# Routing 4,096 tokens to eight experts: one-hot marks made eight picks at a time, router weights held stationary

## The reference, cut to what matters

```python
logits = jnp.einsum('btc,ce->bte', x, router_w) + router_b      # 8 experts, x layer-normalised
top_k_logits, expert_indices = jax.lax.top_k(logits, 2)
expert_probs = jax.nn.softmax(top_k_logits, axis=-1)
one_hot = jax.nn.one_hot(ei, E, dtype=jnp.int32)                # ei: first picks of all tokens, then second
pos = jnp.cumsum(one_hot, axis=0) * one_hot - 1                 # slot of a pick in its expert
expert_inputs = buf.at[ei.ravel(), pos.ravel()].add(xr)         # 1,228 slots for each expert
```

## Time and profile before

| | |
|---|---|
| median of three runs | 2324.01 us |
| the profiled execution, its own time | 2329.72 us |
| its span, first to last instruction | 2328.0 us |
| PE, PEld, DVE, ACT, POOL busy | 2073.9, 1804.6, 1274.3, 1189.6, 500.8 us |
| TensorE clock granted, mean over the span | 0.95 |

### The profile page before, as it was taken

One profiled execution on the slowest core, in us unless ns is written; L12 is line 12 of the kernel. 1 busy time (PEld: TensorE's weight loads), 2 busy tenths in 40 slices (PEclk: granted clock), 3 DMA queues, 4 the chain that ended last, 5 costly groups with the idle time before them and its releaser, 6 DMA issues.

```text
span 2328.0 us, 39168 instructions
## 1 busy us (share of the span) xinstructions
PE 2073.9 (89%) x14589; PEld 1804.6 (78%) x14592; DVE 1274.3 (55%) x2694; ACT 1189.6 (51%) x1926; POOL 500.8 (22%) x728
## 2 busy tenths in 40 slices
PE   5479999999996899999999999984799999999990
PEld 5258888888986678888888788872598899988890
DVE  4555555555555557575575764735445554555544
ACT  1145556655653656465565664611446655675530
POOL 5621111011102212022021100136211101111327
PEclk9999999999998899999999999965799999999995
DMA  5122321222122000000000000030222221222214
GB/s 159 44 77 84 99 79 65 75 86 93 48 89 63 26 8 20 5 15 15 6 19 8 13 1 1 2 126 3 77 58 72 90 72 47 87 95 86 73 59 145
DMA packets 84179, 133.18 MB, mean 57 GB/s; under 512 B 10200, under 2 KB 65824, under 8 KB 84064
## 3 DMA queue, kind: packets, MB, share of 16 engines
q1 hardware_dynamic: 69472, 94.67, 12.1%
q0 software_dynamic: 14592, 36.93, 5.7%
HBM read 98.84 MB, written 32.70 MB: 57 GB/s over the span
## 4 chain that ended last, share of the span: by engine, by line
PE 76%; PEld 7%; POOL 7%; DVE 3%; issue 3%; ACT 2%; DMA 1%; PEldq 1%; DVEq 0%; SPq 0%; POOLq 0%
PE bank L598 28%; PE bank L617 12%; PE bank L669 12%; PE bank L762 4%; PEld bank L617 4%; POOL route_space L450 4%; PEld bank L598 3%; PE bank L745 3%; PE bank L695 3%; PE bank L750 3%; PE bank L717 3%; PE bank L564 2%; POOL halves L466 2%; PE bank L730 2%; PE bank L704 1%
## 5 line engine op out<-in xcount | busy, mean ns | idle before, releaser
L598 PE MATMUL bank<-halves 128*128 128x512 f32 (+2 forms) x3744 | 774.4, 367 | 22.8 <-DVE halves L1186 22.8
L598 PEld LDWEIGHTS bank<-halves 128*128 128x128 f32 x3744 | 651.6, 191 | 129.8 <-issue 25.1
L617 PE MATMUL bank<-halves 128*128 128x256 f32 (+1 forms) x3288 | 403.1, 283 | 3.1 <-issue 3.1
L617 PEld LDWEIGHTS bank<-halves 128*128 128x128 f32 (+1 forms) x3288 | 397.3, 189 | 5.8 <-issue 4.9
L856 ACT ACTIVATE temp<-bank,bias_now 128x512 f32<-128x512 f32 (+1 forms) x312 | 200.2, 642 | 372.4 <-PE bank L598 372.1
L431 POOL DMA_INDIRECT wide<-normed,spare x160 | 164.6, 1029 | 901.0 <-PE bank L579 859.3
L1199 DVE SCALAR_TENSOR_TENSOR temp<-bank,bias_fc,temp 128x512 f32<-128x512 f32 (+1 forms) x312 | 216.1, 693 | 230.1 <-ACT temp L856 226.5
L669 PE MATMUL bank<-halves 128*128 128x512 f32 x1152 | 285.7, 399 | 3.3 <-DVE halves L1327 2.0
L1206 DVE TENSOR_TENSOR halves<-temp,halves 128x512 fp32r<-128x512 f32 (+1 forms) x312 | 198.0, 635 | 126.4 <-ACT halves L815 123.4
L815 ACT ACTIVATE halves<-bank 128x512 fp32r<-128x512 f32 (+1 forms) x176 | 90.1, 545 | 330.0 <-PE bank L579 215.4
L669 PEld LDWEIGHTS bank<-halves 128*128 128x128 f32 x1152 | 211.9, 189 | 51.3 <-DVE halves L1327 2.4
(11 more groups left out here) (174 smaller groups left out, 2338.0 us busy)
## 6 DMA issues: line engine op xcount, KB each, us to landing
expert_out<-rows SPq DMA_DIRECT2D x144, 128.0 KB, 1.7
wide<-in_L_ffn_w_c_fc SPq DMA_DIRECT2D x16, 1024.0 KB, 5.6
wide<-in_L_ffn_w_gate SPq DMA_DIRECT2D x16, 1024.0 KB, 7.6
wide<-in_L_ffn_w_c_proj SPq DMA_DIRECT2D x16, 1024.0 KB, 5.4
normed<-wide SPq DMA_DIRECT2D x8, 1024.0 KB, 4.4
x<-in_L_attn_x SPq DMA_DIRECT2D x4, 1024.0 KB, 9.5
out_x<-x SPq DMA_DIRECT2D x32, 128.0 KB, 2.4
wide<-normed,spare POOLq DMA_INDIRECT x160, 2.8
```

Source lines behind the costliest of these rows:

```text
L598: m = pe.matmul(bank[at + b][:, 0:w], a[:, kc, j * P:(j + 1) * P], v[:, kc, 0:w], start=(i == 0), stop=(i == len(ps) - 1))
L617: mm = pe.matmul(bank[4 + t % 2][0:m, 0:C], a[:, j, o:o + m], v[:, j, :], start=(k == 0), stop=(k == len(ps) - 1))
```

## The change

It does three things.

- **Normalising** is all VectorE's, batch by batch, as soon as a batch's reciprocal is there; `by_pool` and `wait_normed` go. `set_constants` (three memsets) moves ahead of the batches. ScalarE takes the third batch's root one supertile earlier.
- **Logits**: the router's weights are the stationary operand (128x8, two halves of the channels) and the turned tokens move, 512 columns at a time, into an [8, 512] result. ScalarE copies that to `logits_by_expert`, and TensorE turns it back tile by tile to the old place. The turn of supertile s-1 is issued behind the logits of s.
- **Marks**: `row16` and `list16` are the row and the list in bfloat16. Eight picks at a time, VectorE compares lists (`here`, 8x80) and rows (`by_row`, 8x128) and multiplies `here` with the tile's number; ScalarE multiplies `here` with the row's own number. TensorE waits once for eight picks.

The diff, cut to its core:

```diff
-                    for s in (2 * q, 2 * q + 1):
-                        wait_normed(sp, r, s)
+                    sp.wait_ge(xn_made, r * TILES + (q + 1) * QT)
...
-                    for i in range(first, first + tiles):
-                        if by_pool(r, i // SUPER):
-                            nc.gpsimd.tensor_scalar(xn[:, i, :], x[:, i, :], stats[:, i, 1:2], rstd[:, i:i + 1],
-                                                    ALU.subtract, ALU.mult).then_inc(xn_made_pool, 1)
...
-                for j in range(PICKS):
-                    nc.gpsimd.tensor_scalar(by_list[:, j, LISTS:2 * LISTS], index16[:, 0:LISTS], list_of[:, j:j + 1], own,
-                                            ALU.is_equal, ALU.mult).then_inc(own_marked, 1)
...
+                def logits_of(s):
+                    pe.wait_ge(xnt_copied, (r * NSUP + s + 1) * KC)
+                    if s >= 2:
+                        pe.wait_ge(by_expert_copied, r * NSUP + s - 1)
+                    for kc in range(KC):
+                        m = pe.matmul(bank[3 + s % 2][0:E, :], router[:, kc, :], xnt[s % 2][:, kc, :],
+                                      start=(kc == 0), stop=(kc == KC - 1))
+                    m.then_inc(by_expert_done, 1)
+
+                def turn_logits(s):
+                    pe.wait_ge(by_expert_copied, r * NSUP + s + 1)
+                    for b in range(SUPER):
+                        i = s * SUPER + b
+                        m = pe.transpose(bank[(2, 5)[i // HT]][:, i * E:(i + 1) * E],
+                                         logits_by_expert[0:E, s % 2, b * P:(b + 1) * P], ident[0:E, 0:E])
+                    m.then_inc(logits_done, 1)
 
                 turn_xn(0)
                 for s in range(NSUP):
                     if s + 1 < NSUP:
                         turn_xn(s + 1)
-                    pe.wait_ge(xnt_copied, (r * NSUP + s + 1) * KC)
-                    for b in range(SUPER):
-                        i = s * SUPER + b
-                        for kc in range(KC):
-                            m = pe.matmul(bank[(2, 5)[i // HT]][:, i * E:(i + 1) * E], xnt[s % 2][:, kc, b * P:(b + 1) * P],
-                                          router[:, kc, :], start=(kc == 0), stop=(kc == KC - 1))
-                    m.then_inc(logits_done, 1)
+                    logits_of(s)
+                    if s:
+                        turn_logits(s - 1)
+                turn_logits(NSUP - 1)
...
-                        if s == (0, 1, 4)[n]:
+                        if s == (0, 1, 3)[n]:
                             deviation(r * len(BATCHES[0]) + n + 1, slice(first, first + tiles))
                     act.wait_ge(xn_turned, r * NSUP + s + 1)
                     for kc in range(KC):
                         copy(xnt[s % 2][:, kc, :], bank[6 * (s % 2) + kc][:]).then_inc(xnt_copied, 1)
+                    act.wait_ge(by_expert_done, r * NSUP + s + 1)
+                    copy(logits_by_expert[0:E, s % 2, :], bank[3 + s % 2][0:E, :]).then_inc(by_expert_copied, 1)
                 act.wait_ge(gap_made, (r + 1) * HALVES)
                 nc.scalar.activation(weight2[:], weight2[:], ACT.Exp).then_inc(exp_made, 1)
+                for n in range(PICKS // MARKS):
+                    at = slice(n * MARKS, (n + 1) * MARKS)
+                    act.wait_ge(lists_marked, r * PICKS // MARKS + n + 1)
+                    nc.scalar.activation(by_list[:, at, LISTS:2 * LISTS], here[:, at, :], ACT.Copy,
+                                         scale=own).then_inc(own_marked, 1)
...
-                for j in range(PICKS):
-                    v.tensor_scalar(by_row[:, j, :], index16, row_in_tile[:, j:j + 1], None,
-                                    ALU.is_equal).then_inc(rows_marked, 1)
-                    v.tensor_scalar(by_list[:, j, 0:LISTS], index16[:, 0:LISTS], list_of[:, j:j + 1], float(j % TILES),
-                                    ALU.is_equal, ALU.mult).then_inc(lists_marked, 1)
+                for n in range(PICKS // MARKS):
+                    at = slice(n * MARKS, (n + 1) * MARKS)
+                    first = n * MARKS % TILES
+                    v.tensor_tensor(here[:, at, :], index16[:, 0:LISTS].unsqueeze(1).to_broadcast([P, MARKS, LISTS]),
+                                    spread(list16[:, at], LISTS), ALU.is_equal).then_inc(lists_marked, 1)
+                    v.tensor_tensor(by_row[:, at, :], index16.unsqueeze(1).to_broadcast([P, MARKS, P]),
+                                    spread(row16[:, at], P), ALU.is_equal).then_inc(rows_marked, 1)
+                    dve.wait_ge(lists_marked, r * PICKS // MARKS + n + 1)
+                    v.tensor_tensor(by_list[:, at, 0:LISTS], here[:, at, :], spread(index16[:, first:first + MARKS], LISTS),
+                                    ALU.mult).then_inc(tiles_marked, 1)
```

More of the change, by code:

```diff
@@ L186, in macaron @@
         own = part(spare, LISTS, 1)
+        here = part(route_space, 21504, PICKS * LISTS // 2).bitcast(BF16).rearrange("p (j n) -> p j n", n=LISTS)
+        row16, list16 = (room(2424 + PICKS // 2 * n, PICKS // 2).bitcast(BF16) for n in range(2))
+        MARKS = 8
+        logits_by_expert = room(2496, 2, 512)
         v_sb = part(wide, 0, SUPER, HEADS * DH)
@@ L309, in macaron @@
         tok = "(i p) c -> p i c"
-        def by_pool(r, s):
-            return s < 6 if r == 0 else s % 2 == 1
-        def wait_normed(eng, r, s):
-            for pooled, made in ((False, xn_made), (True, xn_made_pool)):
-                n = sum(by_pool(a, b) == pooled for a in range(r + 1) for b in range(NSUP if a < r else s + 1))
-                if by_pool(r, s) == pooled:
-                    eng.wait_ge(made, n * SUPER)
         @block.sync
@@ L433, in load_rows @@
                                                 ).then_inc(xg_loaded[n % 2], 16)
[L435 to L451 removed]
+                if r:
+                    pool.wait_ge(stats_made, 2 * TILES)
+                nc.gpsimd.iota(index, [[1, P]], base=0, channel_multiplier=0,
+                               allow_small_or_imprecise_dtypes=True).then_inc(index_made, 1)
+                pool.wait_ge(index_made, 2 * r + 1)
+                nc.gpsimd.tensor_copy(index16, index).then_inc(index_made, 1)
                 pool.wait_ge(tokens_made, r + 1)
@@ L547, in make_lists @@
                     for j in range(PICKS):
-                        n = r * PICKS + j + 1
-                        pe.wait_ge(rows_marked, n)
-                        pe.wait_ge(lists_marked, n)
-                        pe.wait_ge(own_marked, n)
+                        if j % MARKS == 0:
+                            n = (r * PICKS + j) // MARKS + 1
+                            pe.wait_ge(rows_marked, n)
+                            pe.wait_ge(tiles_marked, n)
+                            pe.wait_ge(own_marked, n)
                         m = pe.matmul(bank[0][:, 0:2 * LISTS], by_row[:, j, :], by_list[:, j, :],
@@ L1046, in inverse_deviation @@
                 dve.wait_ge(std_made, n)
-                v.reciprocal(rstd[:, tiles], rstd[:, tiles]).then_inc(rstd_made, 1)
-                dve.wait_ge(rstd_made, n)
+                steps.after(v.reciprocal(rstd[:, tiles], rstd[:, tiles]))
             def choose(of, k, h):
@@ L1105, in make_lists, with spread @@
                 steps.after(v.tensor_scalar(part2, pos, float(CAP), float(SKIP), ALU.is_ge, ALU.mult))
-                v.tensor_tensor(list_of, part1, part2, ALU.add).then_inc(lists_known, 1)
-                dve.wait_ge(lists_known, r + 1)
+                v.tensor_copy(row16, row_in_tile).then_inc(lists_known, 1)
+                v.tensor_tensor(list16, part1, part2, ALU.add).then_inc(lists_known, 1)
+                dve.wait_ge(lists_known, 2 * r + 2)
                 dve.wait_ge(index_made, 2 * r + 2)
-                for j in range(PICKS):
-                    v.tensor_scalar(by_row[:, j, :], index16, row_in_tile[:, j:j + 1], None,
-                                    ALU.is_equal).then_inc(rows_marked, 1)
-                    v.tensor_scalar(by_list[:, j, 0:LISTS], index16[:, 0:LISTS], list_of[:, j:j + 1], float(j % TILES),
-                                    ALU.is_equal, ALU.mult).then_inc(lists_marked, 1)
+                def spread(t, n):
+                    return t.unsqueeze(2).to_broadcast([P, MARKS, n])
+                for n in range(PICKS // MARKS):
[8 more added lines that the diff above has]
+                                    ALU.mult).then_inc(tiles_marked, 1)
             def route(r):
@@ L1128, in route @@
                     inverse_deviation(r * len(BATCHES[0]) + n + 1, slice(first, first + tiles))
-                set_constants()
-                for s in range(NSUP):
-                    if not by_pool(r, s):
+                    for s in range(first // SUPER, (first + tiles) // SUPER):
                         normalise(s)
```

21 lines of the change are left out of this document (6 added, 15 removed).

## The result

The changed kernel takes 2263.44 us (median of 4 runs, 2262.36 to 2264.71), the kernel before, beside it on the same chip and in the runs shown, 2326.91 (4 runs, 2321.48 to 2329.9): a ratio of 0.973, with a 95% interval of 0.971 to 0.975. The forecast was 2269, with a range of 2258 to 2302; the saving is 63.5 us against the kernel before beside it, where 55.0 was forecast. The profiled execution took 2263.52 us, 66.2 less than that of before (2329.72).

| | before | after | saved | forecast |
|---|---|---|---|---|
| routing 0: choice of the second half | 67.34 | 54.65 | 12.7 | 10.3 |
| choice to first mark | 11.94 | 12.04 | -0.1 | 0 |
| first mark to list | 41.98 | 22.36 | 19.6 | 19.0 |
| list to the experts' first turn | 11.02 | 12.34 | -1.3 | 0 |
| that turn to the first turn of routing 1 | 1408.6 | 1403.65 | 5.0 | 0 |

What follows compares the result with a forecast made beforehand. The experts' matmuls hold most of the span and cannot gain; in each routing everything behind the list waits for it. Savings of 38.2 + 10.3 + 6.5 = 55.0 us take the median from 2324.0 to 2269, range 2258 to 2302.

Steps and rivals of the forecast that it cites:

- The marks: Both routings, first mark to list: 23.0 us in place of 41.98 and 42.22, so minus 38.2 us.
- price of 1.08 ns an element: VectorE's two-input work in the marks: 1.08 ns an element with 0.06 us fixed, eight picks 2.67 us.
- the tail between the last product and the list: End of the marks: TensorE's last eight matmuls are not hidden, between 1.0 and 2.3 us, taken as 1.5.
- Rival 2: Marks: VectorE handles two elements a cycle, 10.0 us more gained in each routing, 2249 us; chance 0.05.
- Normalising and logits: Both routings before the choice: 10.3 us gained in routing 0 and 6.5 in routing 1, minus 16.8 us.
- the rise of the clock: TensorE in both routings: denser moving columns lift it from 1.2 GHz, halving turns, logits and turns back.
- the ring of ScalarE's copy: Per supertile at the high clock: logits 1.8, copy by expert 0.6, next two copies 1.1, hand-overs 0.3: 3.8 us.
- the upper bound: New logits of a supertile, priced like turns of float32 columns: 3.6 us at the low clock, 1.8 at the high.
- the queued splitting: ScalarE's splitting of weights, now queued behind its marks: 8 copies in 4.25 us, at no cost.
- Rival 1: Both routings: the clock stays at 1.2 GHz, 6.2 us a supertile, gain only 23.7 us, 2300 us; chance 0.24.
- Rival 3: Marks: VectorE at two cycles an element, eight picks 5.2 us, marks 43.1, 1 us more than before; chance 0.03.
- rival 4: Marks: the change does not free the path, as ScalarE's marks cost over 2.67 us; no chance given.

Runs made afterwards that it cites:

- old-marks run: Against the changed kernel, only the marks put back: one pick at a time, own marks on GpSimd; 2300.88 us, ratio 0.990.
- dense layout: Against the changed kernel, marks laid out with the pick innermost in memory, for VectorE's three operations; 2256.36 us, ratio 0.971.
- table of four kernels: All with the new marks; normalising shared, logits old 2287.1 us or new 2280.5; normalising on VectorE, logits old 2268.3 or new 2263.4.
- run of the marks alone: Against the kernel before, only the marks changed, with normalising, logits and the third root as before; 2287.12 us, ratio 0.983.

## Why the prediction was right, and where it was off

**The marks (forecast 38.2, measured 39.5).** Right in size and in its reason. The price of 1.08 ns an element from the earlier trace rows was 1.04, eight picks 2.61 us for 2.67, and the tail between the last product and the list, taken as 1.5 us, took 1.43 (87.62 to 89.05), 1.28 of it idle. The nearest row with two inputs was a good guide although it has another type; that the price came so close is in part luck, as it was drawn between two different operations, statistics and a subtraction. ScalarE's mark took 0.83 us for 0.7, and its splitting began at 86.52, before VectorE's, so nothing came late there; the old-marks run shows that 37.4 us of it reach the end. Rival 2 was rightly given little here: the layout of this change runs at 1.04 ns an element, and the dense layout, at 0.52, shows what it would have needed.

**Normalising and logits (forecast 16.8, measured 22.7).** Here the sum was 5.9 us short, and the reason incomplete. The prediction laid the gain on the rise of the clock. The clock did rise, and the ring of ScalarE's copy that it expected closed, but the table of four kernels gives VectorE's normalising 15 to 19 us and the new form, with the clock that stands at 1.00 under it, 5 to 8. What the prediction lacked is that these went into one term and that VectorE's taking over was given no price of its own: with it and the old form, at the low clock for most of both routings, the kernel takes only 4.9 us more. The trace of before held the hint: behind GpSimd's first supertile TensorE began at 19.9 us, behind VectorE's it begins at 15.91, and with the work shared TensorE waits for GpSimd again later (3.56 us ahead of the turn at 43.05 in the run of the marks alone). What made the number short are three sizes within the term; in routing 1 the first two are 2.0 and 1.4 of the 3.5 us:

- The ring is 3.51 us a supertile, forecast 3.8: seven of them, 2.0 us. The logits took the upper bound, as chosen: 1.88 us at the high clock, and 3.58 at the low one in the run that shares normalising. ScalarE's copy took 0.59.
- The clock rose after two turns and part of the first logits (2.62 us in routing 0, 2.16 in routing 1), not behind them; in routing 0 it fell twice in the gaps where TensorE waits for VectorE (0.57 between 24 and 28 us, 0.50 between 36 and 38) and rose again. Forecast had the first logits at 3.6.
- With GpSimd silent, 32 tiles are normalised in 10.43 us, 0.33 each; with it working 16 took 6.72, 0.42. The forecast took 0.39 and bounded it by 0.26 and 0.43.

**The rest.** That the halves' choice, the memsets and the queued splitting cost nothing held: choice to first mark grew by 0.1 us. From the list to the first turn routing 0 took 1.3 us more, which no term had. For the profiled execution the forecast was 2274.7, and 2263.52 came out, 11.2 less: 7.2 from the stages above, 5.0 between the routings, and little else but the 1.3 lost. The 5.7 us by which the profiled execution of before lay above its median were taken off in the forecast already, which leaves 5.6 between 2269 and the result. It lies closer than the saving does (63.5 for 55.0) because the kernel before ran 2.9 us slower beside the change than in the median that the forecast starts from.

**The rivals.** Rival 1 (low clock) did not occur, but its price a supertile is seen in the run that shares normalising: 1.97 us a turn and 3.58 us the logits where the clock is low. Rival 3 was out: 1.04 ns an element is far from 1.72. So was rival 4: ScalarE's marks take 0.83 us, not over 2.67.

## What to carry to other kernels

When a change moves work between engines and also gives it another form, price the two apart: here the clock caught the eye, and the plain fact that VectorE normalises a supertile in 1.3 us where GpSimd takes 4.8 was worth two to three times as much. A layout that makes one engine quicker can make its reader slower: look at who reads each operand before choosing which one gets the stride. And where an engine will start cold behind a wait, idle time can be filled with matmuls that nobody reads: here 7.2 us, with the clock at the high level from the first turn.

## What the runs showed that was not expected

- TensorE's granted clock rose or fell with different work before it, PE being shown busy in each case: it rose among turns of 128 columns (72 in 10.24 us, 0.225 each at the low clock); it stood at 1.00 while logits of 512 columns for 8 loaded alternated with turns; it fell while logits of 8 columns for 128 loaded did (0.92, then 0.50), and in the marks with 160 columns in steps of 16 bytes for 128 loaded (1.00, 0.76, 0.50).
- A moving operand in bfloat16 that steps by 16 bytes took twice as long (0.29 for 0.15 us), the same step on the stationary operand left the matmul as it was (337 for 333 ns) and lengthened its load (163 for 138 ns). The Trainium skill (Advanced Engine Details and Errata, "SBUF Cachelines") says that reads are slowed when each falls in another line of 16 bytes; the trace agrees for the moving operand and for ScalarE, whose copy with an input of such steps took 1.47 for 0.83 us; for the stationary operand the 25 ns of the load are all that shows.
- An output in bfloat16 that steps by 320 bytes made a two-input VectorE operation six times as slow as the same inputs with a packed output (2.94 for 0.49 us).
